# A graph network's row gathers on GpSimd: a memset behind every second gather in place of every gather

## The chip, the cores and the metric

One core of one Trainium2 chip. The metric is the device time of one execution in microseconds (us); lower is better. The kernel before was run three times, and its time is the median.

## The reference, cut to what is computed

Two layers over a graph with 3125 nodes of 256 features and 53,125 edges, sorted by target. In the first, each of 4 heads projects every node to 16 numbers; each edge's logit is the product of its source's and its target's projection, and a softmax over the edges into one target weighs the sources.

```
h = maximum(layernorm(x), 0)
ZU = einsum('nd,kdr->knr', h, U)
zs, zd = ZU[:, src], ZU[:, dst]
logits = (zs * zd).sum(-1) / sqrt(R)
alpha = softmax of logits over the edges of each dst
agg = segment_sum(alpha[..., None] * zs, dst)
ssa = einsum('k,knr,kdr->nd', softmax(head_w), agg, U)
Z_half = 0.5 * h + 0.5 * ssa
x = x + relu(Z_half + ETA * (residual of Z_half) @ Dmat - ETA * LAM)
h = maximum(layernorm(x), 0)
red = segment_sum(h[src] + relvectors[edge_type], dst)
x = x + gru_cell(red, h)
```

## The kernel before, in words

The nodes are cut into NW = 25 windows of W = 125 targets. The edges into a window lie together, since they are sorted, and fit into C = 18 tiles of 128 edges. KR = 64 is the projection of a node over all heads.

The start (to about 58 us): x is loaded and normalised, TensorE projects it, and the projections go to `zu_table` in memory, one row of 64 numbers a node. GpSimd finds the edges of each group of targets with 5 indirect DMAs of line 763 and 10 of line 771, each one row of 125 and back to back. `src_col` holds the source node of each edge, one column a tile.

The stage of gathers (to about 741 us): GpSimd runs `source_rows(t)` for t = 0 to 24. For each of the 18 tiles it issues one indirect DMA (line 698), which fetches the 128 rows of `zu_table` that one column of `src_col` names, into `zs[t % 3]`. There are three such buffers; two are parts of the tensor that the profile calls `shared`, the third is `zs_third`. A window's gathers are in three chunks of 8, 8 and 2 tiles, each with a semaphore of its own (`g_zs`). Window t may only start when VectorE has weighted the rows of window t - 3 (`V_made`), since it uses its buffer. Behind each gather stands a memset of `idle` (lines 702 and 703): the last 300 columns of 54 partitions of `cnt_rows`, a region whose values nobody reads in this stage. It waits for the memset before it by the semaphore `idle_set` and sets nobody else free.

The others work on the window beside it. TensorE picks the targets' rows by a matmul with one-hot columns (line 1747); VectorE multiplies them with the gathered rows, chunk by chunk (line 1010), and sums to logits `L` (line 1013); TensorE turns the logits (line 1754), VectorE finds each target's maximum by scans (lines 1036 to 1044), ScalarE takes the exponential, VectorE weighs the rows (line 1055, the end of the use of `zs[t % 3]`), and TensorE sums them per target with one-hots (line 1772). The first layer's result, the second layer's input and part of the GRU follow in the same loop. The order on each engine is written out by hand; no scheduler moves anything. SP loads and stores by its own queue (a window's edge targets for the one-hots, 1125 KB, each window).

The stage behind (to the end): the second layer, with neighbour sums by matmuls (lines 1846 to 1893, 1865 and 1866 the large ones) and the GRU. It issues no gather: GpSimd has nothing to do.

The lines that matter, of `source_rows`:

```
nc.gpsimd.indirect_dma_start(
    out=zs[t % 3][:, j * KR:(j + 1) * KR], out_offset=None, in_=zu_table,
    in_offset=bass.IndirectOffsetOnAxis(ap=src_col[:, t, j:j + 1], axis=0),
).then_inc(g_zs[t % 3][c], 16)
pool.wait_ge(idle_set, t * C + j + 1)
nc.gpsimd.memset(idle, 0.0).then_inc(idle_set, 1)
```

Of the kernel before, what the change touches and what calls it, by code (L numbers as in the profile page):

```python
# [24 lines left out]
def gnn_kernel(nc, x, edges, U, Dmat, head_w, rel, w_ih, w_hh, b_ih, b_hh, out):  # L25
# [9 lines left out]
    W, C = WINDOW, TILES  # L35
# [20 lines left out]
    with ctx:  # L56
# [3 lines left out]
        def sem(name):  # L60
            return ctx.enter_context(nc.semaphore(name))
# [45 lines left out]
        idle = cnt_rows[0:3 * C, N - 300:N]  # L107
# [182 lines left out]
        idle_set = sem("idle_set")  # L290
# [375 lines left out]
        def _(pool):  # L666
# [23 lines left out]
            def source_rows(t, i, h):  # L690

                if t % GRP == 0:
                    pool.wait_ge(a_col, 3 * (t // GRP) + 1)
                if t >= 3:
                    pool.wait_ge(V_made, t - 2 + CREDIT)
                for c, (a, b) in enumerate(CHUNKS):
                    for j in range(a, b):
                        nc.gpsimd.indirect_dma_start(  # L698
                            out=zs[t % 3][:, j * KR:(j + 1) * KR], out_offset=None, in_=zu_table,
                            in_offset=bass.IndirectOffsetOnAxis(ap=src_col[:, t, j:j + 1], axis=0),  # L700
                        ).then_inc(g_zs[t % 3][c], 16)
                        pool.wait_ge(idle_set, t * C + j + 1)
                        nc.gpsimd.memset(idle, 0.0).then_inc(idle_set, 1)  # L703

            def windowed():
                pool.sem_inc(idle_set, 1)
                pool.wait_ge(st_zu, 16 * 2 * 5)
                each_window(source_rows)
# [1319 lines left out]
```

## Time and profile before

| What | us |
|---|---|
| Median of 3 runs | 1112.35 |
| Lowest and highest | 1110.08, 1118.23 |
| The profiled execution | 1117.96 |
| Its span, first to last instruction | 1115.9 |
| Last memset of the stage of gathers begins | 740.5 |

The span is what the profile's rows cover; the execution's own time is 2.1 us longer. Durations come from this one execution, and it lies 5.6 us above the median. A row of a timeline has the start from the span's beginning, the duration, the engine, the line, the operation, and in brackets the idle time of the engine before it with what ended it. "issue" means that the profile shows nothing that the engine waited for. A gather's row is the engine's part of it; when its data has landed is seen at the reader.

### The profile page before, as it was taken

What the parts mean: (1) busy time and instruction counts of PE and PEld (TensorE: products, weight loads), DVE (VectorE), ACT (ScalarE), POOL (GpSimd) and SP (SyncE); (2) the same over time, 40 slices, a digit from 0 to 9 for tenths busy, and PEclk for the clock granted to TensorE, in tenths of its full rate; (3) what the DMA queues carried; (4) which work ended last, traced back from release to release, by engine and by line L of the source; (5) the groups of instructions that cost most, each with busy time, mean ns of one, the idle gap of its engine ahead of it and who ended that gap; (6) DMA issues with size and microseconds to landing.
All of it is one profiled execution on the core that took longest, in us unless ns stands there. A gap on an engine that the chain in (4) does not pass through costs nothing.

```text
span 1115.9 us, 14910 instructions
## 1 busy us (share of the span) xinstructions
PE 810.7 (73%) x5278; PEld 575.4 (52%) x5278; DVE 650.1 (58%) x1208; ACT 424.5 (38%) x765; POOL 640.3 (57%) x943
## 2 busy tenths in 40 slices
PE   4833466777776655665566565757999999999996
PEld 4722354455544433444444443535777777777774
DVE  4351664655554444455455444645888878888852
ACT  3523233334344333333333333414444444444441
POOL 4688888888888888888888888840000000000000
PEclk9966656767776667667766676679999999999998
DMA  8262335344443434334334333111111111111111
GB/s 188 63 142 58 71 81 120 84 95 86 98 94 97 103 83 89 83 87 96 87 85 95 86 85 87 42 32 42 65 51 47 46 51 48 51 51 56 47 46 35
DMA packets 46513, 85.26 MB, mean 76 GB/s; under 512 B 11246, under 2 KB 29299, under 8 KB 43309
## 3 DMA queue, kind: packets, MB, share of 16 engines
q1 hardware_dynamic: 28898, 66.88, 18.7%
q0 software_dynamic: 16480, 17.31, 12.6%
q8 instruction: 44, 0.72, 0.3%
q14 instruction: 35, 0.29, 0.1%
q10 hardware_dynamic: 1056, 0.07, 0.1%
HBM read 67.29 MB, written 16.80 MB: 75 GB/s over the span
## 4 chain that ended last, share of the span: by engine, by line
POOL 55%; PE 31%; issue 8%; DMA 2%; DVE 2%; SPq 1%; ACT 1%; ACTq 0%; POOLq 0%; DVEq 0%
POOL shared L698 27%; POOL cnt_rows L703 15%; POOL zs_third L698 13%; PE bank L1866 12%; PE bank L1865 6%; PE bank L1892 4%; PE bank L1846 4%; PE bank L1893 2%; DMA layer<-in_edges,row_at 1%; PE bank L1808 1%; SPq L463 1%; SPq L465 1%; PE bank L1889 1%; DMA shared<-in_edges 1%; PE bank L1884 0%
## 5 line engine op out<-in xcount | busy, mean ns | idle before, releaser
L698 POOL DMA_INDIRECT shared<-zu_table,src_col x306 | 301.7, 986 | 53.8 <-issue 49.8
L703 POOL MEMSET cnt_rows<- 54x300 f32 x450 | 165.0, 367 | 0.4
L698 POOL DMA_INDIRECT zs_third<-zu_table,src_col x144 | 143.3, 995 | 23.5 <-issue 23.5
L1772 PE MATMUL bank<-layer,oh 128*125 128x84 f32 x900 | 134.7, 291 | 9.5 <-issue 5.1
L1772 PEld LDWEIGHTS bank<-layer,oh 128*125 128x125 f32 x900 | 120.0, 203 | 21.3 <-issue 14.1
L1010 DVE TENSOR_TENSOR layer<-shared,bank 128x512 f32<-128x512 f32 (+1 forms) x51 | 28.2, 554 | 154.3 <-DMA shared<-zu_table,src_col 115.8
L1754 PE MATMUL bank<-ident,L 128*72 128x128 f32 x75 | 19.2, 382 | 128.1 <-DVE L L1013 121.2
L965 DVE TENSOR_TENSOR shared<-iota_b,key_col 128x1500 bf16<-128x1500 bf16 (+2 forms) x47 | 88.5, 1883 | 0.0
L1808 PE MATMUL bank<-whhT,h2T_own 128*125 128x512 f32 x100 | 88.1, 979 | 0.0
L965 DVE TENSOR_TENSOR oh<-iota_b,low_col 128x3125 bf16<-128x3125 bf16 x25 | 85.2, 3410 | 0.0
L1754 PEld LDWEIGHTS bank<-ident,L 128*72 128x72 f32 x75 | 9.4, 150 | 133.7 <-DVE L L1013 125.3
L1468 ACT ACTIVATE shared<-shared,node_id 125x2304 f32<-125x2304 int32 x25 | 55.4, 2215 | 50.9 <-remote 42.2
L1866 PE MATMUL bank<-wide,zus 125*125 125x512 bf16 x208 | 73.4, 384 | 0.0
L1846 PEld LDWEIGHTS bank<-shared,oh 128*125 128x125 bf16 x625 | 60.0, 138 | 24.3 <-ACT zus L1521 7.2
L1846 PE MATMUL bank<-shared,oh 128*125 128x125 bf16 x625 | 66.3, 223 | 5.6 <-issue 3.2
L1866 PE MATMUL bank<-wide,shared 125*125 125x512 bf16 x192 | 66.9, 379 | 0.0
L1747 PE MATMUL bank<-zu,shared 125*128 125x64 bf16 x1350 | 50.3, 199 | 17.5 <-issue 13.3
L946 DVE SCALAR_TENSOR_TENSOR oh<-iota_w,win_first,bank 128x2250 f32<-128x2250 f32 x24 | 61.2, 2548 | 0.0
L1747 PEld LDWEIGHTS bank<-zu,shared 125*128 125x128 bf16 x1350 | 47.6, 102 | 23.6 <-issue 20.3
L1542 ACT ACTIVATE layer<-layer 125x512 f32<-125x512 f32 x25 | 15.8, 631 | 115.2 <-DVE layer L1154 115.2
L1521 ACT ACTIVATE zus<-bank 125x500 bf16<-125x500 f32 (+1 forms) x91 | 58.4, 686 | 1.6
L1521 ACT ACTIVATE shared<-bank 125x500 bf16<-125x500 f32 (+1 forms) x84 | 54.6, 688 | 6.8 <-PE bank L1846 5.2
(233 smaller groups left out, 1718.0 us busy)
## 6 DMA issues: line engine op xcount, KB each, us to landing
shared<-in_edges SPq DMA_DIRECT2D x25, 1125.0 KB
own_table<-own_out SPq DMA_DIRECT2D x25, 375.0 KB
shared<-own_table SPq DMA_DIRECT2D x25, 375.0 KB
shared<-zu_table,src_col POOLq DMA_INDIRECT x306
h_table<-h2s SPq DMA_DIRECT2D x25, 125.0 KB
h2s<-h_table SPq DMA_DIRECT2D x25, 125.0 KB
out_dram<-layer SPq DMA_DIRECT2D x25, 125.0 KB
xs<-in_x SPq DMA_DIRECT2D x5, 560.0 KB
```

What stands on the lines that cost most here:

```text
L698: nc.gpsimd.indirect_dma_start(out=zs[t % 3][:, j * KR:(j + 1) * KR], out_offset=None, in_=zu_table, in_offset=bass.IndirectOffsetOnAxis(a ...
L703: nc.gpsimd.memset(idle, 0.0).then_inc(idle_set, 1)
L946: nc.vector.scalar_tensor_tensor(o, in0, win_first[:, bass.ds(t, 1)], col, ALU.add, ALU.is_equal).then_inc(oh_made, 1)
L965: nc.vector.tensor_tensor(to.rearrange("p (g w) -> p g w", g=BW)[:, a:b, :], io, col[:, t * BW + a:t * BW + b].unsqueeze(2).broadcast_to([ ...
L1468: nc.scalar.activation(away, dst_bc[h], ACT.Abs, bias=node_id[0:W, t:t + 1], scale=-1.0).then_inc(away_made, 1)
L1521: nc.scalar.activation(many[t % 2].rearrange("p (a g d) -> p g a d", a=NW, g=BW)[:, a:b, :, :], ps(g % 2, W, 0, (b - a) * W).rearrange("p ...
L1747: last = mm(ps(c, 128, (j - a) * KR, (j - a + 1) * KR), ohT[:, j * 128:(j + 1) * 128], zu3[:, m, :], start=m == 0, stop=m == 2)
L1772: last = mm(ps(5, W, 0, SUMS), oh[:, h, j * W:(j + 1) * W], V[:, j, :], start=j == 0, stop=j == C - 1)
L1808: mm(ps(7, W, 0, 2 * D), rows, whhT[:, c, 0:2 * D], start=False, stop=c == CH - 1)
L1846: last = mm(ps(g % 2, W, (k - a) * W, (k - a + 1) * W), lows[t % 2][:, k * W:(k + 1) * W], keys[t % 2][:, k * W:(k + 1) * W], start=True, ...
L1865: mm(ps(bank, W, 0, D), rows, v[:, 2, :], start=False, stop=False)
L1866: last = mm(ps(bank, W, 0, 2 * D), rows, v[:, 0:2, :].rearrange("p m d -> p (m d)"), start=a == 0, stop=a == NW - 1)
```

## The change

`source_rows` sets the memset, and the wait ahead of it, only behind the gathers with odd j: behind the second, fourth and so on of a window's 18. The count that the wait asks for is halved to fit.

```diff
                         ).then_inc(g_zs[t % 3][c], 16)
-                        pool.wait_ge(idle_set, t * C + j + 1)
-                        nc.gpsimd.memset(idle, 0.0).then_inc(idle_set, 1)
+                        if j % 2:
+                            pool.wait_ge(idle_set, t * C // 2 + j // 2 + 1)
+                            nc.gpsimd.memset(idle, 0.0).then_inc(idle_set, 1)
```

GpSimd's instructions at the first window, before. `shared` is the buffer `zs[0]`, a DMA of line 698 is one gather, and `cnt_rows` is the region of the memset.

```order
L698 DMA shared<-zu_table,src_col 128x64 [waits a_col,st_zu]
L703 MEMSET cnt_rows 54x300 [waits idle_set]
L698 DMA shared<-zu_table,src_col 128x64
L703 MEMSET cnt_rows 54x300 [waits idle_set]
L698 DMA shared<-zu_table,src_col 128x64
L703 MEMSET cnt_rows 54x300 [waits idle_set]
```

The same place after; "x2" is two gathers in a row, and the memset's line is now 704.

```order
L698 DMA shared<-zu_table,src_col 128x64 [waits a_col,st_zu]
L698 DMA shared<-zu_table,src_col 128x64
L704 MEMSET cnt_rows 54x300 [waits idle_set]
L698 DMA shared<-zu_table,src_col 128x64 x2
L704 MEMSET cnt_rows 54x300 [waits idle_set]
L698 DMA shared<-zu_table,src_col 128x64 x2
```

Gather and memset took turns before; now two gathers follow each other directly, and one memset stands behind each pair. All 25 windows have this pattern, and the other engines' instructions stand as they stood.

## Rows read from the trace of the kernel before

**Rows 1.** The page of the kernel before: head and busy time of the engines

```profile
span 1115.9 us, 14910 instructions
## 1 busy us (share of the span) xinstructions
PE 810.7 (73%) x5278; PEld 575.4 (52%) x5278; DVE 650.1 (58%) x1208; ACT 424.5 (38%) x765; POOL 640.3 (57%) x943
```

**Rows 2.** The page: 40 slices of the span, 27.9 us each

```profile
POOL 4688888888888888888888888840000000000000
PEclk9966656767776667667766676679999999999998
```

**Rows 3.** The page: chain that ended last, shares by engine and line

```profile
## 4 chain that ended last, share of the span: by engine, by line
POOL 55%; PE 31%; issue 8%; DMA 2%; DVE 2%; SPq 1%; ACT 1%; ACTq 0%; POOLq 0%; DVEq 0%
POOL shared L698 27%; POOL cnt_rows L703 15%; POOL zs_third L698 13%; PE bank L1866 12%; PE bank L1865 6%; PE bank L1892 4%; PE bank L1846 4%; PE bank L1893 2%; DMA layer<-in_edges,row_at 1%; PE bank L1808 1%; SPq L463 1%; SPq L465 1%; PE bank L1889 1%; DMA shared<-in_edges 1%; PE bank L1884 0%
```

**Rows 4.** Timeline of GpSimd from 350 us: start us, us, what [idle before]

```profile
350.34 0.95 POOL L698 DMA_INDIRECT shared<-zu_table,src_col  x1 [0.16 <-issue]
351.29 0.36 POOL L703 MEMSET cnt_rows<- 54x300 f32 x1
351.82 0.95 POOL L698 DMA_INDIRECT shared<-zu_table,src_col  x1 [0.16 <-issue]
352.77 0.36 POOL L703 MEMSET cnt_rows<- 54x300 f32 x1
353.30 0.95 POOL L698 DMA_INDIRECT shared<-zu_table,src_col  x1 [0.16 <-issue]
```

**Rows 5.** Groups of GpSimd: count | busy us, mean ns | idle before

```profile
L698 POOL DMA_INDIRECT shared<-zu_table,src_col x306 | 301.7, 986 | 53.8 <-issue 49.8 <-ACT kind_col L1385 4.0
L703 POOL MEMSET cnt_rows<- 54x300 f32 x450 | 165.0, 367 | 0.4
L698 POOL DMA_INDIRECT zs_third<-zu_table,src_col x144 | 143.3, 995 | 23.5 <-issue 23.5
...
L763 POOL DMA_INDIRECT layer<-in_edges,row_at x5 | 6.7, 1350 | 4.2 <-DVE row_at L805 3.0 <-issue 1.2
L771 POOL DMA_INDIRECT oh<-in_edges,dst_at x5 | 6.0, 1191 | 13.6 <-DVE src_at L817 12.4 <-issue 1.2
L771 POOL DMA_INDIRECT oh<-in_edges,src_at x5 | 5.9, 1190 | 1.5 <-issue 1.5
```

**Rows 6.** Line 698: duration ns min/median/max, and whom it waits for

```profile
L698 POOL DMA_INDIRECT shared<-zu_table,src_col x306: 951/953/2777, 57.9 to 739.6; - x153
L698 POOL DMA_INDIRECT zs_third<-zu_table,src_col x144: 951/953/1777, 115.3 to 712.5; - x144
...
  issue: 73.3, 449
  ACT kind_col L1385: 4.0, 1
```

**Rows 7.** Waits of all engines: us in total, times, longest us

```profile
DVE layer L1010 <- DMA shared<-zu_table,src_col: 115.8, 22, 11.1
...
DVE layer L1010 <- DMA zs_third<-zu_table,src_col: 52.4, 10, 12.1
```

**Rows 8.** Timeline of VectorE in one window: its product waits for gathers

```profile
460.32 0.69 DVE L1010 TENSOR_TENSOR layer<-zs_third,bank 128x512 f32<-128x512 f32 x1 [2.03 <-PE bank L1747]
...
467.23 0.69 DVE L1010 TENSOR_TENSOR layer<-zs_third,bank 128x512 f32<-128x512 f32 x1 [5.44 <-DMA zs_third<-zu_table,src_col]
...
474.00 0.29 DVE L1010 TENSOR_TENSOR layer<-zs_third,bank 128x128 f32<-128x128 f32 x1 [5.37 <-DMA zs_third<-zu_table,src_col]
```

**Rows 9.** Timeline of GpSimd: gathers with no memset, then the first ones

```profile
29.12 1.20 POOL L771 DMA_INDIRECT oh<-in_edges,dst_at  x1 [12.41 <-DVE src_at L817]
30.62 1.18 POOL L771 DMA_INDIRECT oh<-in_edges,dst_at  x1 [0.30 <-issue]
32.11 1.20 POOL L771 DMA_INDIRECT oh<-in_edges,dst_at  x1 [0.30 <-issue]
...
42.59 1.18 POOL L771 DMA_INDIRECT oh<-in_edges,src_at  x1 [0.30 <-issue]
43.77 5.70 POOL L781 DMA_DIRECT2D zu_table<-zus  x8
...
57.87 1.04 POOL L698 DMA_INDIRECT shared<-zu_table,src_col  x1 [4.00 <-ACT kind_col L1385]
58.91 0.37 POOL L703 MEMSET cnt_rows<- 54x300 f32 x1
59.45 1.00 POOL L698 DMA_INDIRECT shared<-zu_table,src_col  x1 [0.18 <-issue]
```

**Rows 10.** Two stretches of 100 us: busy us of each engine, clock, DMA

```profile
core 0 of [0], span 1115.9 us
...
350.00:450.00 100.00, 58.07 (x444) 40.64 (x442) 47.08 (x111) 36.52 (x61) 89.18 (x132) 0.72 0.41 93
850.00:950.00 100.00, 100.00 (x665) 71.97 (x665) 81.70 (x94) 44.64 (x78) 0.00 (x0) 1.00 0.15 48
```

**Rows 11.** Timeline of GpSimd: a gather that took longer

```profile
363.68 1.15 POOL L698 DMA_INDIRECT zs_third<-zu_table,src_col  x1 [0.16 <-issue]
364.82 0.37 POOL L703 MEMSET cnt_rows<- 54x300 f32 x1
365.36 1.78 POOL L698 DMA_INDIRECT zs_third<-zu_table,src_col  x1 [0.16 <-issue]
```

## The prediction, written before the changed kernel ran

> **What bounds the kernel now.** I read the head of the page first. The profiled execution took 1117.96 us, its span is 1115.9 us [rows 1], so 2.1 us lie around it. No engine is busy for much more than 70% of it on average, which says that the kernel has stages. The 40 slices show them: GpSimd is 80% busy from slice 3 to slice 26 and after slice 27 does nothing at all [rows 2]. The chain of waits says who sets the pace: GpSimd holds 55% of the span, its gathers of line 698 27% and 13%, and the memset of line 703 alone 15%, which the change halves [rows 3]. So the changed instruction stands on the path, and its length is no guess.
>
> Next I look at how GpSimd spends that stage. A period is gather 0.95 us, memset 0.36 us directly behind it, 0.16 us of idle time put down to issue, next gather; from start to start 351.82 - 350.34 = 1.48 us [rows 4]. The gather's median is 953 ns in both groups [rows 6], the memset's mean 367 ns over 450 of them [rows 5], and the gathers waited for something else than issue a single time, for the columns from ScalarE at the very start [rows 6]: the gap is 73.3 / 449 = 0.163 us. The wait of a window's first gather for the weighted rows of three windows before costs nothing. GpSimd works back to back from 57.87 [rows 9] for 450 x 1.48 = 666 us, and the long gathers add (986 - 953) x 306 + (995 - 953) x 144 = 16 us [rows 5, 6]: 682 us, to about 740 us. What is left, 1115.9 - 740 = 375 us, holds no gather; TensorE is 100% busy there at the full clock, 2.4 GHz (1.00), against 58% at 0.72 in the stage of gathers [rows 10].
>
> Who follows? VectorE's product of line 1010 waited 115.8 + 52.4 = 168 us for gathers [rows 7]; in one window it stood idle 5.4 us before the second chunk and 5.4 us before the third [rows 8]. So a GpSimd that is faster by some 2 us a window would be followed at once, and a slower one costs its whole loss.
>
> **The change, part by part.** Removed: 9 of the 18 memsets of each window, 225 in all, with 225 waits for the semaphore that counts the memsets. Each wait was for the memset before it on the same engine, long done, so they cost nothing. Kept: 225 memsets in the same form, all 450 gathers, their order and semaphores. No queue is passed by anything, no wait is added, and no other engine reads the memset's columns in this stage. What changes is the spacing: 225 gathers stand directly behind a gather. In a row of before such a pair doesn't exist for the gathers of line 698, so the price needs bounds.
>
> First the pair that stays: gather, memset, gather, 0.953 + 0.364 + 0.163 = 1.481 us from start to start (0.364 from [rows 4], the rest above).
>
> Lower end: the gather keeps its 0.953 us, and the next one starts as a gather behind a gather starts elsewhere on this engine: 0.30 us later [rows 9]. 0.953 + 0.302 = 1.255 us, 0.226 us less than now; 225 x 0.226 = 51 us less. It is not the full memset (225 x 0.364 = 82 us), because the idle time before a gather is 0.16 us behind a memset and 0.30 us behind a gather.
>
> A value inside: the one gather of line 698 with no memset ahead of it, the first, took 1.04 us after 4 us of idle time [rows 9]. With it the pair takes 1.347 us, 0.134 us less: 225 x 0.134 = 30 us less.
>
> Nearest row by its neighbours: the only gathers that the trace has back to back are the ten of line 771. They take 1.191 and 1.190 us on average [rows 5] with 0.30 us between them: 30.62 - 29.12 = 1.50, 32.11 - 30.62 = 1.49 [rows 9]. Mean 1.191 + 0.302 = 1.493 us; with the memset the gather of line 698 has 1.481. The two periods agree within 1%, though the parts differ: 0.24 us more gather and 0.14 us more gap stand against 0.36 us of memset. Taken so, the memset lies in time that a gather needs anyway, and its removal gives 225 x (1.493 - 1.481) = 2.7 us more.
>
> Upper end: the five gathers of line 763, back to back too, while the loads of x run on SP's queue: mean 1350 ns [rows 5]. 1.350 + 0.302 = 1.652, 0.171 us more: 225 x 0.171 = 38 us more.
>
> Between the two ends, 51 us less and 38 us more, I take the value of line 771: ten rows of the same operation with no memset between them, in a steady rhythm. What speaks against it is that those gathers are of another form (125 rows of 132 or 128 elements out of the edge list, against 128 rows of 64 elements), and that the first of them, after 12.4 us of idle time, took 1.20 us too [rows 9]: it had no predecessor to pay for. That is why this case gets barely more than the others.
>
> What the recorded ends leave out matters here. A gather's successor of the same kind starts 0.30 us after its end, while a plain DMA and a memset start at its end (43.77 is 42.59 + 1.18; 351.29 is 350.34 + 0.95) [rows 4, 9]. The Trainium skill says in "Perfetto Trace Analysis", section "DMA Instruction — SWDGE (GPSIMD)", that the recorded end is the last descriptor's, and that the core finishes the instruction after it. By that rule work goes on behind the end, and the memset can be what covers it; without the rule the sum would be the lower end's, 51 us less.
>
> Sum: span 1115.9 + 2.7 = 1118.6, time 1120.7 for the profiled execution. That execution lay 5.6 us above the median of 1112.35 and inside 1110.08 to 1118.23; set against the median the forecast is 1112.35 + 2.7 = 1115 us.
>
> **The rivals.** First, the memset is a plain cost. The row for it: the share of 15% in the chain, the constant 953 ns of 450 gathers, and the first gather of line 771, as long after idle time as behind a gather. Against it: the near equality of the two periods. It has two sizes. At 1.255 us a pair the gathers end 51 us earlier: 1112.35 - 51 = 1061 us. At 1.347 us: 1112.35 - 30 = 1082 us. GpSimd would then still hold VectorE in every window, since 9 x 0.226 = 2.0 us a window is less than the 5.4 us of a single wait [rows 8]. The Trainium skill has a rule for the larger size, in "GPSIMD Engine Reference", section "2.1 Instruction dispatch": consecutive instructions are no barrier between GpSimd's cores, each starts the next as soon as its share is done. By it the idle time of 0.16 behind a memset against 0.30 behind a gather is the next gather's start already running under the memset's end, nothing else hides in it, and the removal gives 1061 us. The trace bears it out in the two gaps, but has no pair to show it.
>
> Second, on the other side: a gather that follows too soon pays more than the memset did. The place is the descriptor work of the second gather of each pair. Gathers take longer where something ahead is not drained: 1.78 and 1.15 us beside the usual 0.95 [rows 11], up to 2.78 us [rows 6], and the back-to-back ones of line 763 have a mean of 1.35 us beside heavy loads. In the stage of gathers every window has loads on SP's queue too. At that price it comes to 1112.35 + 38 = 1151 us. It decides from 1.179 us for the unspaced gather (1.481 - 0.302) on, and leaves the band of 1% from 1.228 us (11.1 us / 225 = 0.049 us more). Against it: today only 16 us in 682 are such delay.
>
> Third, the change might not do what it says. The order shows that it does: half of the memsets are gone and nothing else moved. I give this no chance.
>
> **How the numbers follow.** Forecast case, within 1% of before: 0.35. The memset as a plain cost: 0.35, of which 0.20 for about 1061 us and 0.15 for about 1082 us. The unspaced gather dearer: 0.30, mostly between 1124 and 1151 us. A measurement of this kernel tells about 1% from no change, 11 us. The forecast's own range is 1104 to 1124 us. The wide range takes in the lower size of the plain cost and the upper end of the dear gather: 1060 to 1151 us; what lies outside is a cost above that of line 763, or a gap below 0.30 us. Faster by over 1% 0.35, within 1% 0.35, slower by over 1% 0.30.
>
> **What would show it.** In the changed kernel's timeline of GpSimd, look at the gather directly behind a gather and at the one behind a memset. Forecast right: two starts with no memset between are 1.48 to 1.50 us apart, the recorded gather being near 1.19 us, the gap before it 0.30 us; GpSimd's last instruction ends near 743 us, and the product's waits for gathers stay near 168 us. Plain cost right: 0.95 us and 0.30 us, last instruction near 690 us, waits down by some 40 us. Dear gather right: means above 1.23 us, last instruction beyond 755 us. If the gather behind a memset changes its own 953 ns, all three are incomplete, since the sum moves 225 gathers only. If the stage behind the last gather is not 375 us long, TensorE's clock or its work moved, which no case foresees.

## The result and the profile after

The changed kernel took 1069.33 us (median of 4, 1064.12 to 1072.27) against 1113.44 us (median of 4 runs of the kernel before, three of them those of the section on its time): ratio 0.9588, 95% interval 0.9544 to 0.9631, so between 41 and 51 us less. The forecast was 1115 us and no change. Its wide range held the time, but the likeliest case was the wrong one. The experiments also found something that no part of the prediction foresaw: in other sessions the same changed kernel takes 1302 to 1312 us, 14 to 17% more than the kernel before.

First the page of the changed kernel: the head, the slices of GpSimd and the chain, answering to [rows 1 to 3].

```profile
span 1066.8 us, 14685 instructions
...
POOL 4678888888888888888888888700000000000000
...
POOL 50%; PE 33%; issue 11%; DMA 2%; DVE 2%; SPq 1%; ACT 1%; POOLq 0%; ACTq 0%; DVEq 0%
POOL shared L698 28%; POOL zs_third L698 13%; PE bank L1867 13%; POOL cnt_rows L704 8%; PE bank L1866 6%; PE bank L1893 5%; PE bank L1847 4%; PE bank L1894 2%; DMA layer<-in_edges,row_at 1%; PE bank L1809 1%; SPq L463 1%; SPq L465 1%; PE bank L1890 1%; DMA shared<-in_edges 1%; PE bank L1885 1%
```

GpSimd still sets the pace of the stage of gathers, and the memset's share of the chain fell from 15% to 8%. Then the timeline of GpSimd, one pair with the gathers on either side of the memset, and below it the groups (count | busy us, mean ns | idle before), answering to [rows 4, 5].

```profile
353.50 0.94 POOL L698 DMA_INDIRECT zs_third<-zu_table,src_col  x1 [0.30 <-issue]
354.45 0.36 POOL L704 MEMSET cnt_rows<- 54x300 f32 x1
354.98 0.95 POOL L698 DMA_INDIRECT zs_third<-zu_table,src_col  x1 [0.16 <-issue]
356.23 0.94 POOL L698 DMA_INDIRECT zs_third<-zu_table,src_col  x1 [0.30 <-issue]
```

```profile
L698 POOL DMA_INDIRECT shared<-zu_table,src_col x306 | 302.4, 988 | 75.8 <-issue 71.4 <-ACT kind_col L1386 4.4
L698 POOL DMA_INDIRECT zs_third<-zu_table,src_col x144 | 140.8, 978 | 33.7 <-issue 33.7
L704 POOL MEMSET cnt_rows<- 54x300 f32 x225 | 83.7, 372 | 0.1
```

The gather behind a gather begins 0.30 us after the other's end and takes 0.94 us, no more than one behind a memset: 356.23 - 354.98 = 1.25 us from start to start. The account of GpSimd's stage by the groups, before and after: gathers 445.0 and 443.2 us, memsets 165.0 and 83.7, idle time put down to issue 73.3 and 105.1. The sums are 683.3 and 632.0: 51.3 us less, of a span that is 49.1 us shorter. The last rows of GpSimd, and the waits of VectorE's product, which say that VectorE still hurries after GpSimd:

```profile
688.94 0.94 POOL L698 DMA_INDIRECT shared<-zu_table,src_col  x1 [0.30 <-issue]
689.89 0.36 POOL L704 MEMSET cnt_rows<- 54x300 f32 x1
```

```profile
DVE layer L1011 <- DMA shared<-zu_table,src_col: 132.9, 27, 13.0
...
DVE layer L1011 <- DMA zs_third<-zu_table,src_col: 58.1, 15, 8.0
```

### The profile page after: what moved, and what is told of

Same layout as the page of the kernel before. It is cut to its first block, busy times and chain, and to the rows that moved or that the text cites. A ratio compares the mean times of both kernels' runs of the same rounds, so it can differ in the third digit from the quotient of the medians.

```text
span 1066.8 us, 14685 instructions
## 1 busy us (share of the span) xinstructions
PE 781.0 (73%) x5278; PEld 556.8 (52%) x5278; DVE 648.9 (61%) x1208; ACT 419.9 (39%) x765; POOL 556.9 (52%) x718
## 4 chain that ended last, share of the span: by engine, by line
POOL 50%; PE 33%; issue 11%; DMA 2%; DVE 2%; SPq 1%; ACT 1%; POOLq 0%; ACTq 0%; DVEq 0%
POOL shared L698 28%; POOL zs_third L698 13%; PE bank L1867 13%; POOL cnt_rows L704 8%; PE bank L1866 6%; PE bank L1893 5%; PE bank L1847 4%; PE bank L1894 2%; DMA layer<-in_edges,row_at 1%; PE bank L1809 1%; SPq L463 1%; SPq L465 1%; PE bank L1890 1%; DMA shared<-in_edges 1%; PE bank L1885 1%
## 5 line engine op out<-in xcount | busy, mean ns | idle before, releaser
L698 POOL DMA_INDIRECT zs_third<-zu_table,src_col x144 | 140.8, 978 | 33.7 <-issue 33.7
L1773 PE MATMUL bank<-layer,oh 128*125 128x84 f32 x900 | 104.4, 275 | 0.0
L1773 PEld LDWEIGHTS bank<-layer,oh 128*125 128x125 f32 x900 | 101.4, 191 | 0.1
L1809 PE MATMUL bank<-whhT,h2T_own 128*125 128x512 f32 x100 | 93.3, 1033 | 0.0
L704 POOL MEMSET cnt_rows<- 54x300 f32 x225 | 83.7, 372 | 0.1
L1867 PE MATMUL bank<-wide,zus 125*125 125x512 bf16 x208 | 73.9, 386 | 0.0
L1471 ACT ACTIVATE shared<-shared,ones 125x2304 bf16<-125x2304 f32 x25 | 55.4, 2215 | 0.8
L1748 PE MATMUL bank<-zu,shared 125*128 125x64 bf16 x1350 | 47.4, 199 | 11.1 <-issue 6.3
```

The costliest lines, as they stand in the source:

```text
L698: nc.gpsimd.indirect_dma_start(out=zs[t % 3][:, j * KR:(j + 1) * KR], out_offset=None, in_=zu_table, in_offset=bass.IndirectOffsetOnAxis(a ...
L1471: nc.scalar.activation(ohT, away, ACT.Relu, bias=ones[0:W, :], scale=-1.0).then_inc(oht_made, 1)
L1773: last = mm(ps(5, W, 0, SUMS), oh[:, h, j * W:(j + 1) * W], V[:, j, :], start=j == 0, stop=j == C - 1)
L1809: mm(ps(7, W, 0, 2 * D), rows, whhT[:, c, 0:2 * D], start=False, stop=c == CH - 1)
L1867: last = mm(ps(bank, W, 0, 2 * D), rows, v[:, 0:2, :].rearrange("p m d -> p (m d)"), start=a == 0, stop=a == NW - 1)
```

## The experiments

The runs were made in five sessions. Each session was on one chip and timed the kernel before beside its own kernels. I give the chip's number, because it comes to matter. The line of an instruction moves by a few numbers from kernel to kernel; the names of its tiles stay.

**First session, chip 2, the kernel before at 1115.91 us.** All memsets away:

```diff
-                        if j % 2:
-                            pool.wait_ge(idle_set, t * C // 2 + j // 2 + 1)
-                            nc.gpsimd.memset(idle, 0.0).then_inc(idle_set, 1)
```

> No memset at all behind the 450 gathers. Theory A (the memset is a plain cost; a gather behind a gather starts 0.30 us later and takes its own 0.94 to 0.95 us, whatever stood ahead of it): every period is 1.25 us, another 225 x 0.23 = 51 us go, about 1018 us, as long as VectorE still waits for gathers. Theory B (spacing was worth something that one memset in two still gives: without any, gathers queue behind each other's descriptors and the long ones multiply): GpSimd's periods stay at 1.25 us in the middle, but gathers above 1.1 us rise from 14 us in total to over 40 us, and the time is above 1040 us. Theory C (the others take over as the bound): GpSimd waits for the weighted rows of the window three before, and the time stays between 1030 and 1060 us.

Measured 1007.86 us (ratio 0.9044, 0.901 to 0.9078). This is theory A, with 10 us more gained than it said (1018 us). The groups of GpSimd in this kernel:

```profile
L698 POOL DMA_INDIRECT shared<-zu_table,src_col x306 | 296.8, 970 | 97.3 <-issue 92.9 <-ACT kind_col L1383 4.4
L698 POOL DMA_INDIRECT zs_third<-zu_table,src_col x144 | 140.2, 973 | 43.9 <-issue 43.9
```

Against the changed kernel the memsets are 83.7 us less, the idle time 31.7 us more (136.8), and the gathers 6.2 us less (437.0): 58.2 us less in all. The long gathers did not multiply, so theory B falls; GpSimd waits for nobody, so C falls.

Then a memset of one column behind every gather:

```diff
-                        nc.gpsimd.memset(idle, 0.0).then_inc(idle_set, 1)
+                        nc.gpsimd.memset(idle[:, 0:1], 0.0).then_inc(idle_set, 1)
```

> As before the change, a memset behind every gather, but of 1 column in place of 300. The gap before a gather is 0.16 us behind a memset and 0.30 us behind a gather. Theory A1 (the 0.14 us between the two gaps are the next gather's start, running under any memset's end): the memset takes about 0.1 us, the period is 0.95 + 0.10 + 0.16 = 1.21 us, below the 1.25 us without memset, and the time is about 450 x (1.481 - 1.21) = 122 us below before, 991 us, some 18 us below the kernel with no memset. Theory A2 (those 0.14 us need a memset of that length to hide under): gap and memset together stay at 0.30 us or more, the period is 1.25 us or more, and the time equals that of the kernel with no memset or is above it.

Measured 1010.71 us: theory A2. Its timeline:

```profile
351.30 0.94 POOL L698 DMA_INDIRECT shared<-zu_table,src_col  x1 [0.19 <-issue]
352.23 0.12 POOL L703 MEMSET cnt_rows<- 54x1 f32 x1
352.55 0.94 POOL L698 DMA_INDIRECT shared<-zu_table,src_col  x1 [0.19 <-issue]
```

0.12 + 0.19 is the 0.30 us of a bare gather, one with no memset ahead of it: in these kernels the next gather starts 0.30 us or more after the last one's end whatever stands between, and up to about 0.14 us of a memset lie in that time. That is all that the memset hides.

Two kernels ask why the gathers on which the forecast rested took 1.19 us. Both are made from the changed kernel. In the first each gather fetches 125 of 128 rows from the fourth window on (P is 128 before that), so the last three edges of a tile keep rows of an older window:

```diff
-out=zs[t % 3][:, j * KR:(j + 1) * KR], out_offset=None, in_=zu_table,
+out=zs[t % 3][0:P, j * KR:(j + 1) * KR], out_offset=None, in_=zu_table,
-in_offset=bass.IndirectOffsetOnAxis(ap=src_col[:, t, j:j + 1], axis=0),
+in_offset=bass.IndirectOffsetOnAxis(ap=src_col[0:P, t, j:j + 1], axis=0),
```

> The changed kernel with 125 of the 128 rows in each gather from the fourth window on, so the three last edges of a tile keep rows of an older window. It asks why the gathers of the edge list took 1.19 us, the rows on which the forecast rested. If it is the count of rows (125 does not split over 16 engines evenly), the gathers take 1.19 us and both gaps stay; if it is the form of the table, they stay at 0.94 to 0.95 us.

The gathers have a mean of 1199 ns, and the time rose to 1161.95 us (one run). In the second the table is a flat list of numbers, and each gather fetches 128 rows of the same size from wrong places:

```diff
+            flat_zu = bass.AP(zu_table.tensor, 0, [[1, N * KR], [1, 1]])
-out=zs[t % 3][:, j * KR:(j + 1) * KR], out_offset=None, in_=zu_table,
+out=zs[t % 3][:, j * KR:(j + 1) * KR], out_offset=None, in_=flat_zu,
```

> The changed kernel with the table of projections read as a flat list of numbers, as the gathers of the edge list read theirs: 128 rows of 64 numbers each, but each starting at the number with the node's index and not at 64 times it, so wrong rows are fetched, of the same size. If the flat form is what made the gathers of the edge list take 1.19 us, these take 1.19 us too; if it is the count of 125 rows, they stay at 0.94 to 0.95 us.

1068.36 us (one run), gathers of 979 and 987 ns on average: the flat form costs nothing. The count of 125 rows does. The rows of line 771 are also longer, 128 or 132 numbers against 64, but with 64 numbers the 125 rows already take 1.20 us, no less than the 1.19 us of line 771, so nothing is left for that length. The group of the kernel with 125 rows:

```profile
L699 POOL DMA_INDIRECT shared<-zu_table,src_col x306 | 366.8, 1199 | 77.1 <-issue 73.2 <-ACT kind_col L1387 3.9
L699 POOL DMA_INDIRECT zs_third<-zu_table,src_col x144 | 172.6, 1199 | 34.5 <-issue 34.5
```

The idle time is that of the changed kernel within 3 us. So 0.24 us of the 1.49 us period of line 771 was the price of 125 rows, and its nearness to 1.48 us was chance.

**Second session, chip 6, the kernel before at 1117.76 us.** The memset on other partitions:

```diff
-                        nc.gpsimd.memset(idle, 0.0).then_inc(idle_set, 1)
+                        nc.gpsimd.memset(cnt_rows[64:115, N - 300:N], 0.0).then_inc(idle_set, 1)
```

> As before the change, a memset of 300 columns behind every gather, but on 51 partitions from the 64th on in place of 54 from the first. Theory A (GpSimd takes one instruction after the other, whatever partitions they touch; only the next gather's start runs under a memset's end): gather 0.94 to 0.95, memset 0.36, gap 0.16 us, period 1.48 us, the time of before within 1%. Theory D (a memset that shares no partitions with whatever the gather works on runs beside it, since GpSimd's cores are not held together): the period falls towards that of no memset, 1.25 us, and the time towards 1008 us. Either way the memset lies on the path only if the period says so.

1118.58 us, ratio 1.0006 (0.9983 to 1.0029), period 1.48 us: theory A. A memset of 150 columns (`idle[:, 0:150]`) behind every gather:

> As before the change, a memset behind every gather, but of 150 columns. From 1 column (0.12 us, gap 0.19) and 300 columns (0.36 us, gap 0.16) I get 0.24 us for the memset and 0.16 us for the gap. Theory A (the path's price is memset plus gap, less the 0.30 us that a bare gather pays anyway): 0.24 + 0.16 - 0.30 = 0.10 us a gather, 450 x 0.10 = 45 us above the kernel with no memset, about 1053 us. Theory E (up to some length a memset hides as a whole, and the 300 columns lie beyond it): the period is still 1.25 us and the time about 1008 us.

1064.23 us. Theory A had 1053, theory E 1008. Memsets of 244 ns and gaps of 73.9 us in total give a price of 0.10 us a gather, as expected, so a memset of 150 columns too hides 0.14 us and no more. The other 8.6 us are in the gathers themselves, 445.6 us against 437.0 with no memset; why they are longer stays open. A memset behind every gather in windows 0 to 11 only:

```diff
-                        if j % 2:
-                            pool.wait_ge(idle_set, t * C // 2 + j // 2 + 1)
+                        if t < 12:
+                            pool.wait_ge(idle_set, t * C + j + 1)
                             nc.gpsimd.memset(idle, 0.0).then_inc(idle_set, 1)
```

> As before the change in windows 0 to 11, with no memset in windows 12 to 24: 216 memsets, 9 fewer than the changed kernel has, but none of them alternates with a bare gather. The first half of the memsets brought about 44 to 49 us, the second about 60. Theory A (each memset costs the same 0.226 us wherever it stands, and what was over came from other things, long gathers and the stage behind): 1008 + 216 x 0.226 = 1057 us and up to 8 us more. Theory F (the mixing of spaced and bare gathers in the changed kernel costs something of its own, in longer gathers of the same tile places in each window): this kernel is at 1057 us or below, the changed one at 1069, and the gathers above 1 us are fewer here than there.

The diff is against the changed kernel. 1060.53 us: A's range. Against the changed kernel it has 9 memsets fewer (2 us) and 3 us less in gathers (440.2 against 443.2). Theory F is not excluded for a few us. Gathers of 112 rows (P = 112 in the kernel with 125 rows):

> The changed kernel with 112 of the 128 rows in each gather from the fourth window on, so the last 16 edges of a tile keep rows of an older window. With 125 rows the gather took 1.20 us against 0.95 with 128. If it is the remainder over 16 rows that costs, 112 = 7 x 16 rows take 0.95 us or less; if it is fewer rows than the full 128, or the order of the partitions, they take 1.20 us as well.

1058.06 us (one run); the gathers take 954 and 977 ns on average, with 0.93 us in the timeline. So it is not fewer rows that cost 0.25 us. 112 and 128 are multiples of 16, 125 is not; the three counts fit that as the rule, but three counts don't show it.

**Third session, chip 9, the kernel before at 1114.99 us.** The changed kernel again, and 225 memsets at other places:

```diff
-                        if j % 2:
-                            pool.wait_ge(idle_set, t * C // 2 + j // 2 + 1)
+                        if j < 9:
+                            pool.wait_ge(idle_set, t * (C // 2) + j + 1)
                             nc.gpsimd.memset(idle, 0.0).then_inc(idle_set, 1)
```

> The changed kernel once more, beside the next one on the same chip. From the account by rows its memsets cost 225 x 0.226 = 51 us over the kernel with none, 1008 + 51 = 1059 us; measured were 1069 us. If the 10 us are its own, it gives 1066 to 1071 us again; if they were the other chip or chance, 1058 to 1064 us.

> 225 memsets as in the changed kernel, but behind the first nine gathers of each window and none behind the last nine. Theory A (only the number counts): equal to the changed kernel beside it, within 3 us, each at 1059 to 1064 us. Theory F (the place counts, through the long gathers that meet the loads of SP's queue at the same tiles of each window): it differs from the changed kernel by 5 us or more, and the time that gathers take above their median, 15.7 us there, differs by as much.

Measured 1302.35 us (all six between 1298 and 1309) and 1246.24 us. Neither expectation had room for it: the same program is 233 us slower than when it was first timed. Its gathers are as quick as ever (0.94 to 0.95 us, gap 0.30), yet GpSimd now stands still. Waits of the changed kernel in the third session (engine, line and whom it waited for: us, times, longest):

```profile
DVE den L1104 <- remote: 245.7, 22, 13.6
...
DVE layer L1011 <- remote: 161.6, 53, 8.4
...
POOL shared L698 <- DVE layer L1056: 150.2, 14, 18.2
...
PE bank L1773 <- issue: 83.1, 174, 1.6
POOL zs_third L698 <- DVE layer L1056: 71.6, 7, 11.2
```

GpSimd waits 222 us for the weighted rows of the window three before, a wait that cost nothing before. VectorE in its turn waits for TensorE. "remote" means that a semaphore ended the wait and that no instruction that sets it has its recorded end near that moment. The semaphore that ended these two waits was TensorE's in all 75 cases: that of the summed rows (line 1773) for `den`, that of the picked rows (line 1748) for the product. And TensorE, in the 36 matmuls of a window that sum the rows (line 1773), waits 174 times for nothing that the profile shows. The kernel with memsets behind the first nine gathers of a window shows more of it. Its timeline of TensorE and of GpSimd from 575 us:

```profile
575.77 1.02 PE L1773 MATMUL bank<-layer,oh 128*125 128x84 f32 x3 [0.42 <-issue]
577.20 0.69 PE L1773 MATMUL bank<-layer,oh 128*125 128x84 f32 x2 [0.41 <-issue]
579.32 0.51 PE L1773 MATMUL bank<-layer,oh 128*125 128x84 f32 x2 [1.42 <-issue]
581.43 0.30 PE L1773 MATMUL bank<-layer,oh 128*125 128x84 f32 x1 [1.61 <-issue]
```

```profile
576.10 0.94 POOL L698 DMA_INDIRECT shared<-zu_table,src_col  x1 [0.30 <-issue]
577.35 0.94 POOL L698 DMA_INDIRECT shared<-zu_table,src_col  x1 [0.30 <-issue]
578.60 0.94 POOL L698 DMA_INDIRECT shared<-zu_table,src_col  x1 [0.30 <-issue]
```

Beside bare gathers one to three matmuls are issued every 1.4 to 2.1 us. Below are stretches of the same run, with the busy time of these matmuls alone (stretch, length, busy PE and PEld with counts, clock, DMA share, GB/s). The first is beside gathers with a memset behind each (spaced ones), just after GpSimd had stood still for 15.79 us; the second is beside the gathers of another window, the third is after the last gather of all. The fourth is the start of the second, still beside spaced gathers: the first bare gather there begins at 576.10 us.

```profile
539.00:544.00 5.00, 4.05 (x34) 3.93 (x34) 1.00 0.37 101
571.00:591.00 20.00, 9.45 (x34) 8.20 (x35) 0.50 0.43 90
877.00:881.00 4.00, 3.83 (x35) 3.86 (x36) 1.00 0.31 97
```

```profile
571.00:575.00 4.00, 1.95 (x6) 1.73 (x7) 0.50 0.09 16
```

```profile
536.81 1.02 POOL L698 DMA_INDIRECT shared<-zu_table,src_col  x1 [15.79 <-DVE layer L1056]
```

The same number of matmuls takes 5, 20 and 4 us. DMA traffic is alike in these three, and TensorE is held up already in the fourth, where the 16 DMA engines are busy only 9% of the time; so the total load on them doesn't explain it. A bare gather right beside isn't needed either: of the 20 us the first 4.4 lie beside spaced gathers, behind the bare ones of the window before. And the quick stretch comes behind a pause of GpSimd, so the pair of 5 and 20 us doesn't measure the memsets alone; the fifth session does. The granted clock doesn't explain it either: 0.50 is the level of 1.2 GHz, half the full clock, and the second stretch takes five times as long as the third.

**Fourth session, chip 11, the kernel before at 1118.28 us.** The kernel before, no memset, one column, and the memset on the other partitions, each once more:

> The kernel before, for its trace. In the last two runs (one chip) TensorE's 36 matmuls of line 1773 took 17 to 19 us in windows where only bare gathers ran beside them, 4 to 6 us beside spaced gathers, 3.87 us with no gather beside; in the runs before them (other chips) always 3.87 us. Theory G (a property of the chip on which the call lands: on some, gathers hold up TensorE's supply of instructions, and the memset is what gives it time): if this call lands on such a chip the phase takes 5 to 8 us here and the time stays 1110 to 1120 us, because GpSimd bounds; on the other sort 3.87 us and the same time. Theory H (chance of the moment, not the sort of chip): no relation between this trace and the next three.

> No memset. Theory G: on a chip of the first sort every gather is bare, TensorE's phase takes 17 us or more in every window, GpSimd waits for VectorE's weighted rows, and the time is above the changed kernel's 1302 us; on the other sort 1008 us again. Theory H: 1008 us whatever the trace of the kernel before shows.

> A memset of 1 column behind every gather. If on a chip of the first sort it is the length of the pause between the descriptors of two gathers that lets TensorE go on (0.30 us here as with no memset), it is as slow as the kernel with no memset; if it is the mere fact that another instruction stands between, it is close to 1008 us. On the other sort of chip 1010 us.

> The memset of 300 columns on partitions 64 to 114 behind every gather. If it is the pause that counts, it is like the kernel before, 1110 to 1120 us and TensorE's phase at 5 to 8 us on a chip of the first sort; if the memset has to occupy the part of GpSimd that makes descriptors (the low partitions), it is as slow as with no memset there.

Measured 1116.39, 1012.55, 1011.01 and 1118.18 us: in the fourth session TensorE isn't held up, and all four repeat the first two sessions. Their traces have no such waits. So it wasn't put to the test here whether the memset has to lie on the low partitions.

**Fifth session, chip 11 again, the kernel before at 1155.07 us.** The kernel before, the changed one, no memset, one column:

> The kernel before once more, to read the sort of chip: TensorE's phase of 36 matmuls in 3.87 us beside gathers says that nothing holds it up, 5 us and more (as in the first trace of before) that something does. The time is 1110 to 1120 us either way.

> The changed kernel beside it. If the phase is at 3.87 us in g1: 1062 to 1072 us. If it is at 5 us or more: about 1302 us as before on chip 9, with the phase near 11 us.

> No memset. If the phase is at 3.87 us in g1: 1008 to 1013 us. If it is at 5 us or more: the phase at 17 us or more in every window, and a time above the changed kernel's.

> A memset of 1 column behind every gather. If the phase is at 3.87 us in g1: 1008 to 1014 us. If it is at 5 us or more: as slow as g3 if the length of the pause is what counts, close to 1010 us if any instruction between two gathers is enough.

In the fifth session TensorE is held up, more than in the third. The kernel before takes 1153.73 us, the changed one 1312.26 us (1.1421, 1.1211 to 1.1632), no memset 1385.12 us (1.2056, 1.1834 to 1.2277), one column 1389.70 us. My expectation of 1110 to 1120 us for the kernel before missed: here even the spaced gathers hold TensorE up enough that GpSimd waits 25.5 us for the weighted rows. The group of TensorE's matmuls (count | busy us, mean ns | idle before), in the fifth session: before, changed, no memset.

```profile
L1772 PE MATMUL bank<-layer,oh 128*125 128x84 f32 x900 | 166.0, 330 | 24.6 <-issue 19.0 <-DVE oh L946 0.5
```

```profile
L1773 PE MATMUL bank<-layer,oh 128*125 128x84 f32 x900 | 192.6, 341 | 96.9 <-issue 94.4
```

```profile
L1770 PE MATMUL bank<-layer,oh 128*125 128x84 f32 x900 | 213.4, 357 | 278.4 <-issue 278.3
```

The same group without the hold-up, in the first session's kernel with no memset, and in the fourth session's kernel before:

```profile
L1770 PE MATMUL bank<-layer,oh 128*125 128x84 f32 x900 | 107.1, 280 | 0.0
```

```profile
L1772 PE MATMUL bank<-layer,oh 128*125 128x84 f32 x900 | 107.4, 280 | 0.0
```

Unexplained idle time grows 19, 94, 278 us as the memsets go from 450 to 225 to 0, and one column (307 us) protects no more than none. So another instruction between two gathers is not enough; the time between them counts, 0.53 us with 300 columns against 0.30 or 0.31 us. Whether it is this pause, or that gathers then come every 1.48 us and not every 1.25, no run tells apart. GpSimd's wait for the weighted rows grows with it: 25.5, 228 and 348 us.

Not only TensorE's issue is late, its signals are too. In the kernel with no memset VectorE's product waits 441 us in total, in 42 waits, for the picked rows (line 1745 there, 1747 before). One such place, with TensorE's last record of these matmuls, its burst of sums, and the product:

```profile
612.63 0.28 PE L1745 MATMUL bank<-zu,shared 125*128 125x64 bf16 x4 [0.53 <-issue]
...
632.43 3.66 PE L1770 MATMUL bank<-layer,oh 128*125 128x84 f32 x17 [0.41 <-issue]
```

```profile
632.57 0.69 DVE L1008 TENSOR_TENSOR layer<-shared,bank 128x512 f32<-128x512 f32 x1 [16.95 <-remote]
```

The record says that the picked rows were done by 612.91 us, and VectorE got the signal at 632.5, in the moment in which TensorE ran freely again, 3 us behind GpSimd's last gather of that window (628.34 + 0.94 us). What the records don't settle is whether TensorE worked and couldn't say so, or whether its records are ahead of its work.

| | TensorE free | TensorE held up |
|---|---|---|
| before, 450 memsets | 1116 to 1118 | 1112 (the time before), 1115 (chip 9), 1154 |
| changed, 225 | 1069 | 1302 (chip 9), 1312 |
| no memset | 1008, 1013 | 1385 |
| 1 column | 1011, 1011 | 1390 |

(us; the third and the fifth session are the right column, and the kernel before as it was first timed, for a reason that follows.) The kernel with no memset beats the kernel before by 9 to 10% and the changed one by 5 to 6% in one column and loses to both in the other. No version timed in both columns beats the kernel before in both.

## Why the prediction was wrong

What held. GpSimd bounds the stage of gathers, the memset lies on the path, and VectorE follows at once: the account above and the kernel with no memset show it, for the sessions in which TensorE is free. The lower end was worked out to the point: a pair at 1.255 us, 51 us less, GpSimd's last instruction near 690 us (measured 1.25 us, 51.3 us, 690.3 us). The rival "the memset is a plain cost" named it with 1061 us; the median of 1069 us lies 8 us above. Most of this is the base: the 51 us were read from an execution of 1117.96 us and taken off a median of 1112.35, which is 5.6 us less. Another 1.6 us are in the stage behind the last gather's start, 377.9 us against 376.3. Taken off the execution that was traced, 1117.96 - 51.3 + 1.6 = 1068.3 us, beside 1068.69 measured.

One of its signs failed all the same: the product's waits for gathers were to fall by some 40 us from 168, and they are 191. The base is at fault, as shown below: in the trace of before VectorE also waited for a late TensorE, and so less for gathers. The kernel before with a free TensorE (fourth session) has 248 us, and from there they fell by 57.

```profile
DVE layer L1010 <- DMA shared<-zu_table,src_col: 163.7, 31, 9.6
...
DVE layer L1010 <- DMA zs_third<-zu_table,src_col: 84.2, 15, 12.1
```

GpSimd's own account doesn't hang on this: gathers, memsets and idle time come to 682.5 us there, against 683.3 in the trace of before.

What failed is one step: "Between the two ends [...] I take the value of line 771". I chose the row by its neighbours (no memset between) and set aside that it was of another form. The kernels with 125 rows and the flat table show which part of the form it was: 125 rows cost 0.24 us of gather, which stood against the memset's 0.23 us and made the periods agree within 1%. The text had the row that told otherwise, the first gather of line 771, as long after 12.4 us of idle time as behind a gather; it should have decided. The nearest row is the one whose differences can be priced, and 1.04 us of the first gather of line 698 was nearer: it gave 30 us less. The agreement of two sums whose parts disagree was no evidence.

With it fell the reading that work behind the recorded end is what the memset covers. Of the memset 0.14 us lie under the next gather's start, which shows in the two gaps, and the kernels with one column and with 150 show that there is no more. The rival rested on a rule of the Trainium skill in "GPSIMD Engine Reference", section "2.1 Instruction dispatch": consecutive instructions are no barrier between GpSimd's cores. The sum that the prediction took from it was the right one, and the hidden 0.14 us agree with it. No run shows the cores themselves, though: with the memset on partitions 64 to 114, which was to run beside the gather if this freedom reached that far (theory D), the period stayed at 1.48 us.

The rival on the other side, a gather that pays more for following too soon, was wrong in its place. Gathers of 128 rows behind gathers took 0.94 to 0.95 us in every timeline shown. (Its premise, that a gather is long when something ahead isn't drained, is shown only this far: around the two long ones at 363 to 366 us of the trace of before the DMA engines were busy 0.72 and 0.65 of the time, against 0.41 over 350 to 450 us.) What pays in the third and the fifth session is TensorE, by 278 us of unexplained idle time with no memset, and the prediction never looked there. The trace of before carries the sign, in one row of the group of these matmuls and three of the waits.

```profile
L1772 PE MATMUL bank<-layer,oh 128*125 128x84 f32 x900 | 134.7, 291 | 9.5 <-issue 5.1
```

```profile
DVE den L1103 <- remote: 42.6, 9, 7.6
...
DVE layer L1010 <- remote: 26.8, 12, 4.5
...
PE bank L1772 <- issue: 5.1, 25, 0.4
```

There are 25 waits of TensorE for nothing, in a phase where it has all it needs, and 134.7 us of busy time where the free runs have 104 to 108; and VectorE has "remote" waits. These tell the two sorts of session apart: all seven traces with a held-up TensorE have them, and none of the thirteen others. So the kernel before was profiled with TensorE held up a little, and the changed kernel with TensorE free. In the kernel before that costs nothing there, and how much it would cost with fewer memsets these rows couldn't say. I had read "issue" waits of GpSimd and left TensorE's aside, because it wasn't the bound.

Open is what makes a session one of the one or the other sort. It isn't the chip's number (chip 11 gave both, which speaks against the property of a chip that theory G had), nor the program (the changed kernel and the one with no memset gave both), nor single executions (all six runs of the third session's changed kernel agree within 1%). Which core of the chip ran the program, where its data lay and what ran beside it were not recorded or varied. Open too is by which path gathers hold up TensorE. That they do is shown by the fifth session, where only the memsets differ, and by the windows with no gather left, whose 36 matmuls take 4.14 us in the same runs:

```profile
877.17 4.14 PE L1773 MATMUL bank<-layer,oh 128*125 128x84 f32 x36
```

## What to carry to other kernels

A filler instruction on the bounding engine may be a plain cost there and protection for another engine: before it is taken out, look at the unexplained waits of the engines that aren't the bound, and time the result in several sessions and on several chips, since one session here said 4% faster and another 17% slower. And when an unseen sequence is priced by the nearest row, price each difference of that row; two periods that agree with parts that don't agree say nothing.

## What the runs showed that I had not expected

- Gathers on GpSimd can hold up TensorE's issue and its signals. Busy and idle time of the 36 fp32 matmuls of a window, on average over the 25 windows: 5.8 and 7.6 us with 0.53 us between all gathers (trace of before, fifth session), 11.6 us with 0.53 and 0.30 us by turns, 19.7 us with 0.30 us. In other sessions the same programs show none of it and take 4.3 us.
- A gather of 125 rows takes 1.20 us of GpSimd, one of 128 rows 0.95, one of 112 rows 0.93.
- A memset of one column costs nothing that the times show between two gathers: 0.12 us and a gap of 0.19 replace a gap of 0.30.
